# Causal linear attention inside a 16-layer kernel, rebuilt on the slot pipeline of its sibling stages

## The reference, cut to what matters

```
x = x + attn(layernorm(x))
q, k, v = split(layernorm(x) @ w_attn.T)        # 16 heads, 8 features each
qp, kp  = elu(q) + 1, elu(k) + 1
scores  = where(causal, qp @ kp.T, 0)           # no softmax
y       = (scores @ v) / (scores.sum(-1) + 1e-6)
attn    = y @ w_proj.T
```

## Time and profile before

| | us |
|---|---|
| median of three runs | 3355.29 (3349.27 to 3361.4) |
| the profiled execution | 3366.05 |
| its span | 3364.3 |
| PE busy in the span | 2804.9 (83%) |
| DVE | 2007.6 (60%) |
| ACT | 1387.5 (41%) |
| POOL | 962.4 (29%) |

### The profile page before, as it was taken

The page is one execution under the profiler, slowest core; times in us unless marked ns, Lnnn a source line. Parts: engine busy times, 40 slices in busy tenths (PEclk is TensorE's granted clock), DMA queues, the critical chain, the costliest instruction groups (busy, mean ns, idle before and its releaser), DMA issues. The chain is left out here.

```text
span 3364.3 us, 61234 instructions
## 1 busy us (share of the span) xinstructions
PE 2804.9 (83%) x23920; PEld 1857.1 (55%) x23920; DVE 2007.6 (60%) x4357; ACT 1387.5 (41%) x2886; POOL 962.4 (29%) x1321
## 2 busy tenths in 40 slices
PE   5589699979699969887687699996999969689996
PEld 2233367756477645555454566763566646456664
DVE  4999754556655566733465356665666646556664
ACT  4444244434244333322253244443555524345553
POOL 1355332223323220103213333331122235412222
PEclk7799799989799978777798799997999979799998
DMA  1000100000000000002010000001122101022221
GB/s 77 1 0 0 51 1 1 1 23 27 1 1 1 1 1 1 1 1 83 17 27 17 19 1 1 1 1 52 55 70 80 60 22 33 15 69 77 69 77 43
DMA packets 46939, 90.95 MB, mean 27 GB/s; under 512 B 6052, under 2 KB 34524, under 8 KB 45888
## 3 DMA queue, kind: packets, MB, share of 16 engines
q1 hardware_dynamic: 44608, 86.43, 8.4%
q0 software_dynamic: 2048, 0.61, 0.1%
HBM read 70.16 MB, written 19.14 MB: 27 GB/s over the span
## 5 line engine op out<-in xcount | busy, mean ns | idle before, releaser
L751 ACT ACTIVATE s_sT<-s_R 128x1024 f32<-128x1024 f32 (+2 forms) x448 | 400.1, 945 | 197.9 <-PE s_R L685 197.0
L786 DVE TENSOR_REDUCE s_negm<-s_R 128x4 f32<-128x1024 f32 x320 | 377.1, 1221 | 174.6 <-PE s_R L656 174.6
L656 PE MATMUL s_R<-s_qk 32*128 32x256 f32 (+2 forms) x3584 | 250.1, 394 | 62.7 <-ACT s_sT L751 33.5
L685 PE MATMUL s_R<-s_qA,s_qk 32*128 32x256 f32 (+2 forms) x3584 | 241.5, 383 | 16.1 <-DVE s_negm L786 10.7
L704 PE MATMUL s_OB<-s_sT,s_v 128*32 128x256 f32 (+2 forms) x3584 | 224.6, 368 | 10.0 <-ACT s_sT L751 6.4
L758 ACT ACTIVATE s_oc<-s_OB 128x256 f32<-128x256 f32 x224 | 86.0, 384 | 333.7 <-PE s_OB L704 333.7
L656 PEld LDWEIGHTS s_R<-s_qk 32*128 32x128 f32 x3584 | 158.7, 191 | 110.8 <-issue 88.5
L801 DVE TENSOR_TENSOR s_qA<-s_qk,s_X 128x256 f32<-128x256 f32 x224 | 94.3, 421 | 200.2 <-PE s_X L716 200.2
L2493 POOL TENSOR_TENSOR all_hT<-s0s_hs,s0s_cb 128x1024 f32<-128x1024 f32 x64 | 150.6, 2354 | 199.4 <-DVE s0s_hs L2527 182.2
L685 PEld LDWEIGHTS s_R<-s_qA,s_qk 32*128 32x128 f32 x3584 | 162.9, 185 | 78.4 <-issue 64.1
L1375 POOL TENSOR_TENSOR s_pr<-s_pr,s_rinv 128x1024 f32<-128x1024 f32 x64 | 121.3, 1895 | 224.7 <-DVE s_rinv L1481 224.7
(11 more groups left out here) (571 smaller groups left out, 6284.6 us busy)
## 6 DMA issues: line engine op xcount, KB each, us to landing
s_wB<-enc_b SPq DMA_DIRECT2D x32, 962.5 KB, 4.9
s_scratch<-s_pk SPq DMA_DIRECT2D x51, 256.0 KB, 2.0
s_qk<-s_scratch SPq DMA_DIRECT2D x204, 64.0 KB
s_wA<-enc_a SPq DMA_DIRECT2D x32, 193.0 KB, 4.1
big<-moe SPq DMA_DIRECT2D x2, 2347.0 KB, 11.2
big<-routed SPq DMA_DIRECT2D x2, 2084.0 KB
all_W<-weights SPq DMA_DIRECT2D x1, 2296.0 KB, 17.1
all_W<-weights SPq DMA_DIRECT2D x1, 2295.5 KB, 12.1
```

The lines of the kernel that those rows point to most:

```text
L656: last = pe.matmul(S[h][:, t * T:t * T + hi - lo], b.qk[rows, r % 2, 0, c, t * P:(t + 1) * P], b.qk[rows, r % 2, 1, c, lo:hi], start=(t == ...
L685: last = pe.matmul(b.R[:, a.turned_at(u, h // 2), :][:, h % 2, a.at(kt)], b.qk[rows, r % 2, 1, c, kt * P:(kt + 1) * P], b.qA[rows, u % 2, ...
L751: act.activation(b.sT[:, u % (a.lag + 1), 2 * p:2 * p + 2, 0:a.width], b.R[:, a.turned_at(u, p), 0:a.width], ACT.Exp).then_inc(s.expd, 1)
L786: ins = dve.tensor_reduce(b.negm[:, u % 2, :, at].rearrange("p t h -> p h t"), S.rearrange("p h (t k) -> p h t k", t=TT), AX_X, ALU.max, n ...
```

## The change

The padded weights, the layer norm stage of this layer and the old linear stage go. The new `linear_attention_stage` uses the plan, the buffers' layout and several helpers of the slot stages (`slot_wait_qk`, `slot_x_pe`, `slot_front_pe`, `slot_turn_o_pe`, `slot_project_pe`, `slot_turn_out_pe`, `slot_out_act`, `slot_setup_v_dve`).

- q and k of a batch are one front (two matmuls, one exp, one relu, one join, 512 columns each) and are spread to the row blocks by transfers.
- Scores contract 32 rows of the array in place of 8; the rows between heads are set to zero once.
- Scores go to the ring of three bank pairs. The first pair of heads is masked by DVE out of PSUM (512 and 256 columns); the second is copied by ACT (768 columns) and masked by POOL in SBUF.
- Values lag two units behind the scores, and now stand ahead of the scores in PE's order. They wait for the norm of the unit before (`o_norm`), since values and their transposes share bank OB.
- Norms are made by batch inside the stage.

PE's order in a step u is: values(u-2), early items, scores(u), transposes(u-2), late items. DVE's is: the add of a finished batch, mask(u), norm(u-2), join, moments or scaling of a coming batch. The diff, cut to its core:

```diff
-    def __init__(self, units, early, late, extra, mask=None, first=()):
+    def __init__(self, units, early, late, extra, mask=None, first=(), maxima=True):
...
-            if u + 1 < self.U:
+            if maxima and u + 1 < self.U:
                 order.append(("m", u + 1))
...
+        self.qk = st.sb("qk", [P, 2, 2, a.NC, T])
+        self.pk = st.sb("pk", [P, 2, 2 * T])
+        self.ex = st.sb("ex", [P, 2 * T])
+        self.v = st.sb("v", [P, 2, TT, a.H, 32])
+        self.sT = st.sb("sT", [P, a.lag + 1, a.HP, TT * a.n[0]])
+        self.oc = st.sb("oc", [P, 2, T])
+        self.rden = st.sb("rden", [P, 2, TT, a.HP])
+        self.o = st.sb("o", [P, 2, TT, D])
+        self.oT = st.sb("oT", [P, T])
+        self.R = st.ps("R", [P, 6, 512])
+        self.X = st.ps("X", [P, 512])
+        self.OB = st.ps("OB", [P, 512])
+        self.sems = LinearSems(st)
...
+    early = {2: [("t", -1)], 3: [("y", -1)]}
+    late = {0: [("qk", 1)], 1: [("v", 1)], 3: [("h", 2)]}
+    a = SlotPlan(B, early, late, 5, "causal", [("h", 0), ("h", 1)], maxima=False)
...
+            @block.sync
+            def _(sp):
+                for r in range(B):
+                    sp.wait_ge(s.phi, r + 1)
+                    if r == 0:
+                        sp.wait_ge(s.zeroed, 3)
+                        for c in range(NC):
+                            for h in range(HP):
+                                rows = 32 * c + a.HD * h
+                                sp.dma_start(b.qk[32 * h:32 * h + a.HD, 0, :, c, :],
+                                             b.pk[rows:rows + a.HD, 0, :].rearrange("p (n t) -> p n t", n=2))\
+                                  .then_inc(s.qk_first[c], 16)
+                        continue
+                    if r >= 3:
+                        slot_wait_qk(sp, s, r - 2, 0)
+                    sp.dma_start(scratch[r % 2], b.pk[:, r % 2, :]).then_inc(s.stored, 16)
+                    sp.wait_ge(s.stored, 16 * r)
+                    if r >= 2:
+                        sp.wait_ge(s.scored, 2 * NC * (r - 1))
+                    of = scratch[r % 2].rearrange("(c h e) (n t) -> h e n c t", c=NC, h=HP, n=2)
+                    for h in range(HP):
+                        sp.dma_start(b.qk[32 * h:32 * h + a.HD, r % 2, :, :, :], of[h]).then_inc(s.qk_in, 16)
+
+            @block.gpsimd
...
+                pool.memset(b.qk[:, 1, :, :, :], 0.0).then_inc(s.zeroed, 1)
+                for u in range(U):
+                    pool.wait_ge(s.high_copied, u + 1)
+                    m = diagonal(b.sT[:, u % (a.lag + 1), :, :], 1)
+                    pool.affine_select(out=m, in_=m, compare_op=ALU.is_ge, fill=0.0, base=0,
+                                       pattern=[[0, 2 * TT], [1, P]], channel_multiplier=-1)\
+                        .then_inc(s.high_masked, 1)
...
+                def scores(u):
+                    r, c = divmod(u, NC)
+                    slot_wait_qk(pe, s, r, c)
+                    if u >= 1:
+                        pe.wait_ge(s.low_masked, u)
+                    if u >= 2:
+                        pe.wait_ge(s.high_copied, u - 1)
+                    for kt in range(TT):
+                        lo, hi = a.queries[kt]
+                        for h in range(HP):
+                            rows = slice(32 * h, 32 * (h + 1))
+                            last = pe.matmul(b.R[:, a.pair(2 * u, h // 2), :][:, h % 2, a.at(kt)],
+                                             b.qk[rows, r % 2, 1, c, kt * P:(kt + 1) * P], b.qk[rows, r % 2, 0, c, lo:hi],
+                                             start=True, stop=True, skip_group_check=True, tile_position=(32 * h, 0))
+                            if kt == TT - 1 and h % 2:
+                                last.then_inc(s.scored, 1)
+
+                def values(j):
+                    r, c = divmod(j, NC)
+                    if c == 0:
+                        pe.wait_ge(s.x_used, a.number[("v", r)] + 1)
+                    pe.wait_ge(s.low_masked, j + 1)
+                    pe.wait_ge(s.high_masked, j + 1)
+                    if j:
+                        pe.wait_ge(s.o_norm, j)
+                    for kt in range(TT):
+                        lo, hi = a.queries[kt]
+                        for h in range(HP):
+                            last = pe.matmul(b.OB[32 * h:32 * (h + 1), lo:hi], b.v[:, r % 2, kt, HP * c + h, :],
+                                             b.sT[:, j % (a.lag + 1), h, a.at(kt)], start=(kt == 0),
+                                             stop=(kt == TT - 1), skip_group_check=True, tile_position=(0, 32 * h))
+                    last.then_inc(s.pv, 1)
+
+                for item in a.first:
+                    other(item)
+                for u in a.steps:
+                    j = u - a.lag
+                    if 0 <= j < U:
+                        values(j)
+                    for item in a.early(u):
+                        other(item)
+                    if 0 <= u < U:
+                        scores(u)
+                    if 0 <= j < U:
+                        slot_turn_out_pe(pe, g, a, b, j)
+                    for item in a.late(u):
+                        other(item)
...
+                        act.activation(b.ex[:], b.X[:], ACT.Exp).then_inc(s.bent, 1)
+                        act.activation(b.pk[:, r % 2, :], b.X[:], ACT.Relu).then_inc(s.x_used, 1)
...
+                        act.wait_ge(s.scored, 2 * u + 2)
+                        act.activation(b.sT[:, u % (a.lag + 1), 2:4, 0:a.width], b.R[:, a.pair(2 * u, 1), 0:a.width],
+                                       ACT.Copy).then_inc(s.high_copied, 1)
...
+                def phi(r):
+                    dve.wait_ge(s.bent, r + 1)
+                    dve.wait_ge(s.x_used, a.number[("qk", r)] + 1)
+                    dve.scalar_tensor_tensor(out=b.pk[:, r % 2, :], in0=b.ex[:], scalar=1.0, in1=b.pk[:, r % 2, :],
+                                             op0=ALU.min, op1=ALU.add).then_inc(s.phi, 1)
+
+                def mask_low(u):
+                    dve.wait_ge(s.scored, 2 * u + 1)
+                    for kt in range(TT):
+                        n = a.n[kt]
+                        ins = dve.tensor_tensor(b.sT[:, u % (a.lag + 1), 0:2, a.at(kt)],
+                                                b.R[:, a.pair(2 * u, 0), a.at(kt)],
+                                                g.causal01[:, 0:n].unsqueeze(1).to_broadcast([P, 2, n]), ALU.mult)
+                    ins.then_inc(s.low_masked, 1)
+
+                def norm(j):
+                    r, c = divmod(j, NC)
+                    dve.wait_ge(s.turned, j + 1)
+                    tk = b.OB[:, T:2 * T].rearrange("p (t h e) -> p t h e", t=TT, h=HP)
+                    dve.tensor_scalar(b.rden[:, j % 2, :, :], tk[:, :, :, a.HD], 1e-6, None, ALU.add).then_inc(s.den, 1)
+                    dve.wait_ge(s.den, j + 1)
+                    dve.reciprocal(b.rden[:, j % 2, :, :], b.rden[:, j % 2, :, :]).then_inc(s.recip, 1)
+                    dve.wait_ge(s.recip, j + 1)
+                    if c == 0 and r >= 2:
+                        dve.wait_ge(s.x_mm, a.number[("t", r - 2)] + 1)
+                    dve.tensor_tensor(b.o[:, r % 2, :, 32 * c:32 * (c + 1)].rearrange("p t (h e) -> p t h e", h=HP),
+                                      tk[:, :, :, 0:a.HD],
+                                      b.rden[:, j % 2, :, :].unsqueeze(3).to_broadcast([P, TT, HP, a.HD]), ALU.mult)\
+                       .then_inc(s.o_norm, 1)
...
+                ln.moments_dve(dve, g, 0)
+                ln.moments_dve(dve, g, 1)
+                dve.memset(b.qk[:, 0, :, :, :], 0.0).then_inc(s.zeroed, 1)
+                ln.apply_dve(dve, g, 0)
+                ln.apply_dve(dve, g, 1)
+                slot_setup_v_dve(dve, a, b)
+                phi(0)
+                for u in a.steps:
+                    for what, r in a.early(u):
+                        if what == "y":
+                            dve.wait_ge(s.x_mm, a.number[("y", r)] + 1)
+                            xb = g.x[:, TT * r:TT * r + TT, :]
+                            dve.tensor_tensor(xb, xb, b.X[:, 0:T].rearrange("p (t d) -> p t d", t=TT), ALU.add)\
+                               .then_inc(s.x_used, 1)
+                    if 0 <= u < U:
+                        mask_low(u)
+                    if 0 <= u - a.lag < U:
+                        norm(u - a.lag)
+                    for what, r in a.late(u):
+                        if what == "qk":
+                            phi(r)
                     if (r := a.turns(u, 1)) is not None:
...
-OWN_NORM = ("L0_ffn", "L2_ffn", "L0_attn_b", "L2_attn_b", "L3_attn_b", "L3_ffn")
+OWN_NORM = ("L1_attn_b", "L0_ffn", "L2_ffn", "L0_attn_b", "L2_attn_b", "L3_attn_b", "L3_ffn")
...
-    W.add("L1b_wq", head_chunks(w[:D], 8))
-    W.add("L1b_wk", head_chunks(w[D:2 * D], 8))
+    W.add("L1b_wq", w[:D].T)
+    W.add("L1b_wk", w[D:2 * D].T)
```

(16 more changed lines are left out.)

262 lines of the change are left out of this document (66 added, 196 removed).

## The result

The changed kernel takes 3341.79 us (median; 3337.92 to 3343.54) against 3355.29: ratio 0.9957, interval 0.9941 to 0.9973. The forecast was 3335.3, the range 3322 to 3350; it saves 13.5 us where 20 were forecast. The profiled execution took 3337.92 (span 3336.2), that of before 3366.05. Of these 28.1 us of span the layer gives 14.4 (162.5 to 148.1); 5.6 lie ahead of it and 8.1 behind, in stages that the change doesn't touch. Those parts spread by as much from one execution to the next: over the thirteen traces of this case the time ahead of the layer runs from 1236.3 to 1242.0 us and the time behind it from 1950.2 to 1962.4, and the kernel of e8, which is the old one but for a line, has 1238.0 ahead. So the two profiled executions overstate the change, and the stage alone answers to the medians.

The account below looks back on a forecast made before the run. PE bounds the old stage; afterwards a PE-DVE chain does. Start 17.4, body 115.1 and tail 9.0 give 141.5 us against 162.5; of 21 saved, 1 is taken off, so 3355.29 becomes 3335.3, range 3322 to 3350.

Parts of the forecast that it names:

- Start: From the last write before the stage to the first scores: 17.4 us against 26.6, 9.2 us saved.
- The scaling beside POOL's memset: In the start, all four tiles' scaling on DVE waits for POOL's longer memset: 1.9 us, bounds 0 and 3.
- The relay: PE and DVE take turns in each unit (values, scores, mask, norm): 3.39 us a unit, 14.6 a batch at high clock.
- The boundaries: Between batches, store, wait and four loads take 7.0 us and stay hidden; PE waits on no transfer after the first batch.
- 3.2 us are left: Slack at a batch boundary: store possible 3.5 us after unit 0's scores, transfers 7.0, next scores 13.7 after.
- this sign: Listed as showing the forecast wrong: PE waits for loads at batch boundaries.
- The clock: PE's clock in the body is 0.95 or more after the first 9 us, rising at about 9.5 us.
- Rival 1: In the body the clock falls as often as before: another 26 us low cost 9 us, 3343; chance 0.16.
- Tail: From the end of the last scores, scores(31), to the stage's end: 9.0 us against 9.25.
- Rival 2: The chain of PE and DVE is longer, 0.2 to 0.3 us a unit, 8 us: 3343 to 3347; chance 0.13.
- Rival 3: PE's waits in each unit keep the body's clock at 1.2 GHz: 34 us slower, 3389; chance 0.05.
- the port wait 2: Term of the range's lower end: the start without DVE's wait beside POOL's memset, 2 us.

Follow-up runs that it names:

- e8: The kernel before with scores over all 32 rows of a head's block in place of 8 (output not the reference's): 3345.46 us, ratio 0.9960.
- e10: e1 with POOL zeroing its half of q and k ahead of the inverse roots, small transfers all on SP: 3312.50 us, ratio 0.9866.
- e2: The changed kernel with eight of the first batch's sixteen small transfers issued from ACT's queue in place of SP's: 3344.66 us, ratio 0.9950.
- e7: The changed kernel with scores over the 8 rows that carry data in place of 32: 3379.90 us, ratio 1.0058.
- e4: The changed kernel with all masks on DVE, without ACT's copy of scores and POOL's select: 3383.21 us, ratio 1.0083.
- e1: The changed kernel reordered: PE does transposes and most items ahead of scores, DVE does norm ahead of mask: 3313.74 us, ratio 0.9884.

## Why the prediction was right, and where it was off

Mechanism and sign held, and the time lies in the range; the saving in the stage is 14.4 where 21 stood.

- **Start** 17.4, measured 16.4. The scaling beside POOL's memset, priced at 1.9 us more for all four tiles, held only the second pair (1.86 us; it ended at 1243.08, the memset at 1242.94):

```profile
1241.14 1.80 POOL L819 MEMSET s_qk<- 128x2048 f32 x1
1241.22 1.86 DVE L298 TENSOR_SCALAR all_h<-all_x,s_ln_mv,s_ln_rstd 128x128 f32<-128x128 f32 x2 [0.33 <-POOL s_ln_rstd L291]
```

  The prediction had no term for POOL's inverse root of the second pair: it took 2.06 us beside DVE's memset, for 0.70 of the first. Why isn't shown, as in e10 one beside the same memset took 0.69.

- **The relay.** Right in its order, and right that the removed PE work is worth nothing at the high clock: a batch takes 15.0 against 14.9. The size was off by 0.11 a unit: scores to mask 0.97, mask to norm 0.94, norm to values 0.80, values to scores 0.79, against 0.94, 1.02 less 0.08, 0.72 and 0.79. Two hand-overs were priced 0.03 and 0.08 too low: 3.1 us over the 28 units behind unit 3. PE's own work was priced too high: 12.3 us of a batch, where it is busy 43.4 of 60 us, 10.8 of 15.0.
- **The boundaries.** The step that failed most: "3.2 us are left" was worked out for a steady batch, and there it holds (no wait at any of the six later ones). For batch 1 the sum counted SP's 11.9 us of small transfers only against the units that need them, not against the store queued behind them. From store to scores the transfers took 9.3 us, for the 7.0 that the prediction counted to the last byte. e2 parts the two: its store goes as soon as the join is done, 5.6 us behind the first scores (at the low clock) and not 3.5; the transfers then take 8.5, and PE still waits 0.4. So of the 3.0 us, 1.8 are the queue, 0.8 the slower transfers behind it, and 0.4 would have come anyway. The clock then stood at 0.51 from 1267.6 to 1274.5, and batch 1 took 16.7 for 15.0, 1.7 more. The prediction's own list named this sign.
- **The clock.** Right in its level (0.95 in the body), by analogy with two other stages, and in part by luck: it expected PE busy 0.84 of the time, like the stage at 0.85, and the clock held although PE was busy only 0.72. The reason wasn't understood: the prediction noted that the old stage was at 0.50 with PE busy all 10 us, and that slot stages with 32 rows hold 1.00, but named no cause. Rival 1, that the clock falls as before, is what e7 shows with 8 rows, and there it cost 37 us of stage rather than 9. It rose earlier than chosen: the scores of unit 2 ended 7.6 us into the body, not 9.5.
- **Tail** 9.0, measured 10.9 from the end of the last scores: it fell low again (0.68) as PE idles between the last rounds; values took 1.51 us at 1378.07 for 0.86. No low stretch had been put there, though the old tail had them.
- **Rival 2** (the chain longer, 3343 to 3347) came nearest in time: what was found is its mechanism at half its size, 0.11 us a unit for its 0.2 to 0.3 and one boundary that waits for loads. Rival 3 decided nothing here, but e4 shows that it was one mask away. The saving of 13.5 us lies under the 15 to 26 to which the forecast gave its 0.60, and above what rivals 1 and 2 gave.

Together: start 1.0 better; body 5.7 worse (relay 3.1, wait 3.0, low clock 1.7, less 1.9 for the early rise; 0.2 is rounding); tail 1.9 worse. That is 6.6 of the 21 us, of which the forecast had taken off 1.

The range is looser than its working: the terms named for its lower end (20, the port wait 2, the low stretch 1, the baseline 6) add up to 29 us and not 33. Nothing hangs on it here.

What stays open: why the unchanged stages ahead and behind spread by 6 and 12 us between executions, when the clock rises in the first batch (e1), and why it falls in some tails and not in others. Letting values go without the norm's wait (another bank for the transposes) wasn't tried; e1 makes the wait free instead.

## What to carry to other kernels

When work is taken off the bound engine, write down the relay that two in-order engines run within one unit, and put on each engine first what the other needs next: the same instructions in another order were worth 31 us of stage here, twice the whole change (24 by the ratios). Price a transfer by everything queued ahead of it on its queue, the prologue too. Where matmuls contract few rows, look at the granted clock before counting instructions: filling the row block with zeros costs the matmuls no time (0.94 us a unit at the high clock either way) and may keep the clock up.

## What the runs showed of the hardware that was not expected

- In both kernels the granted clock followed how many rows the matmuls use, and not only PE's busy time: 8 for 32 rows took the body from 0.95 to 0.58 in one kernel (stage +37 us), 32 for 8 from 0.87 to 0.98 in the other (stage -14, and -15 us against the runs beside it), with PE busier in both 8-row kernels. TensorE: Matmul & The Clock Gate, section "HAM oscillation — how this bites in real kernels", of the Trainium skill puts the low clock down to idle gaps of PE; e8 differs from that, since it and the kernel before are equally busy at the high clock (13.7 of a batch's 14.9, and 55.3 of 60).
- Issuing one small transfer of 8 rows holds the issuing queue 0.7 to 0.9 us (SP 4.33 for six, ACT 6.39 for eight, 3.56 for four), and on ACT the compute behind it waits.
